# Splitting expert weights one expert ahead in a fused attention and mixture-of-experts block

## The reference

```python
xn = layernorm(x)                       # x: 4 x 256 tokens, 512 wide
# attention: 32 query heads, 8 key/value heads of 16
q, k, v = xn @ Wq, (xn @ Wkv) split in k and v, each shared by 4 heads
ctx = softmax(mask(q @ k.T) / 4) @ v
attn = ctx @ Wo + bo
# experts: 16 of inner width 256
scores = sigmoid(xn @ gate_w.T) + bias
cw = top-4 of scores, divided by their sum
z = silu(xn @ Wg[e].T) * (xn @ Wu[e].T) * cw[:, e]
out = sum over e of z @ Wd[e].T  +  shared expert
return x + attn + out
```

## Time and profile before

| | |
|---|---|
| median of 3 runs | 566.04 us (565.2 to 567.9) |
| the profiled execution | 569.64 us, span 567.9 us |
| mean granted clock of TensorE | 0.943 |
| busy TensorE, VectorE, ScalarE, GpSimd | 468.4, 365.0, 263.5, 268.3 us |

### The profile page before, as it was taken

The page is one execution under the profiler, slowest core; times in us unless marked ns, Lnnn a source line. Parts: engine busy times, 40 slices in busy tenths (PEclk is TensorE's granted clock), DMA queues, the critical chain, the costliest instruction groups (busy, mean ns, idle before and its releaser), DMA issues.

```text
span 567.9 us, 9993 instructions
## 1 busy us (share of the span) xinstructions
PE 468.4 (82%) x2968; PEld 344.9 (61%) x2968; DVE 365.0 (64%) x606; ACT 263.5 (46%) x386; POOL 268.3 (47%) x234
## 2 busy tenths in 40 slices
PE   0995789968989997789878878997978899889880
PEld 0964578846667775367656655765656557667650
DVE  7377874676567957375779871787775546766510
ACT  2531212216555655165668642655736335645610
POOL 2002593304764652267546863573757336364510
PEclk9997999987998998899999899998989999889976
DMA  7804963336666557465687883668655534334222
GB/s 285 329 28 111 226 231 100 107 118 214 158 130 152 113 104 212 142 157 96 141 236 190 277 162 60 154 139 205 175 104 107 95 56 83 68 54 81 38 38 37
DMA packets 32060, 78.23 MB, mean 138 GB/s; under 512 B 4288, under 2 KB 11200, under 8 KB 28800
## 3 DMA queue, kind: packets, MB, share of 16 engines
q0 software_dynamic: 11936, 27.53, 26.8%
q1 hardware_dynamic: 17808, 43.96, 23.5%
q10 hardware_dynamic: 2256, 6.03, 5.0%
HBM read 54.04 MB, written 23.33 MB: 136 GB/s over the span
## 4 chain that ended last, share of the span: by engine, by line
PE 45%; DVE 15%; issue 8%; DMA 8%; ACT 8%; ACTq 6%; POOL 5%; SPq 2%; DVEq 1%; POOLq 1%
PE psum L1093 24%; PE psum L1221 5%; DMA q_parts<-stage 3%; ACT wsplit L573 3%; DVE negm L906 3%; PE psum L1187 2%; PE psum L1203 2%; POOL xn L446 2%; PE psum L1058 2%; ACTq L266 2%; PE psum L1115 2%; PE psum L1042 2%; POOL out L457 1%; PE psum L1103 1%; ACTq L264 1%
## 5 line engine op out<-in xcount | busy, mean ns | idle before, releaser
L1093 PE MATMUL psum<-wsplit,xgT 128*128 (+1 forms) x660 | 175.0, 416 | 0.2
L1093 PEld LDWEIGHTS psum<-wsplit,xgT 128*128 128x128 f32 x660 | 125.8, 197 | 30.3 <-issue 2.7
L457 POOL DMA_INDIRECT out<-ysb,tab x48 | 88.6, 1845 | 105.1 <-ACT ysb L606 84.2
L1093 PE MATMUL psum<-wsplit,zT 128*128 (+1 forms) x336 | 95.3, 420 | 29.0 <-DVE zT L898 29.0
L1093 PEld LDWEIGHTS psum<-wsplit,zT 128*128 128x128 f32 x336 | 61.6, 193 | 48.9 <-issue 37.6
L948 DVE TENSOR_TENSOR xgT<-psum,xgT 128x512 fp32r<-128x512 f32 x47 | 32.3, 688 | 65.4 <-ACT xgT L569 65.3
L437 POOL DMA_INDIRECT xg<-xn_rows,tab x47 | 51.9, 1104 | 29.6 <-PE psum L1231 20.0
L648 ACT ACTIVATE xn<-psum 128x1536 f32<-128x1536 f32 x32 | 46.5, 1453 | 40.6 <-PE psum L1189 40.6
L975 DVE TENSOR_TENSOR plo<-xn,phi 128x1536 f16<-128x1536 f32 x32 | 63.5, 1984 | 1.0
L446 POOL TENSOR_SCALAR_AFFINE_SELECT xn<-xn 128x512 f32<-128x512 f32 x64 | 55.3, 1060 | 7.9 <-ACT xn L648 7.8
L462 POOL TENSOR_TENSOR wsplit<-wraw,wsplit (+1 forms) x16 | 39.1, 2446 | 41.1 <-ACT wsplit L573 41.1
(11 more groups left out here) (180 smaller groups left out, 655.9 us busy)
## 6 DMA issues: line engine op xcount, KB each, us to landing
wraw<-wexp SPq DMA_DIRECT2D x17, 1024.0 KB, 6.1
wraw<-wexp SPq DMA_DIRECT2D x17, 512.0 KB, 4.6
q_parts<-stage SPq DMA_DIRECT2D x16, 192.0 KB
q_pack<-q_parts ACTq DMA_DIRECT2D x6, 384.0 KB, 4.6
xn<-x SPq DMA_DIRECT2D x4, 512.0 KB, 5.2
xn_rows<-xn SPq DMA_DIRECT2D x8, 256.0 KB, 7.6
ctxs<-x SPq DMA_DIRECT2D x8, 256.0 KB, 3.2
out<-ysb SPq DMA_DIRECT2D x8, 256.0 KB, 3.2
```

Of the source, the lines that this page charges most:

```text
L457: nc.gpsimd.indirect_dma_start(out=out, out_offset=rows_of(s), in_=ysb[:, par, :], in_offset=None, compute_op=ALU.add).then_inc(y_out[par] ...
L1093: last = MM(dst, lhs(a, k), split_weights(place, w, c), start=m == 0, stop=m == len(products) - 1)
```

## The change

The gate/up weights of expert e + 1 are split in the first slot of expert e, not in the last slot before e + 1 begins; its down weights in the slot after that. On ScalarE the splits stand behind `y_evac`, on VectorE behind `low16`. The table now holds the number of the *next* expert at a slot that begins one, the place is worked out from that number, and each engine loads one register value a slot, after `tanh` or `gated`. On GpSimd, too, the register is loaded once. The transposed z goes to bank 3 (`ZB`), and the transposed maxima, after the first, to bank 4 (`NM`, the bank of `weighted`), so the wait for y moves from before `z_transpose` to before `down`, and three waits are added for the new sharing. Three small VectorE operations are added once, to make the table.

```diff
--- before.py
+++ after.py
@@ -250,6 +250,7 @@
 
 
         GU, XT, DN, PV = 5, 6, 7, 4
+        ZB, NM = 3, PV
         WO = (PV, 3)
         TRB = (0, 1, GU, XT)
 
@@ -462,13 +463,18 @@
                 nc.gpsimd.tensor_tensor(wsplit[:, place, 1, PARTS[1]], wraw[:, place, PARTS[1]],
                                         wsplit[:, place, 0, PARTS[1]].bitcast(F32), ALU.subtract).then_inc(w_low[1], 1)
 
-            def down_low_of(s):
-
-                number = pool.value_load(where[0:1, 2, s + 1:s + 2], min_val=0, max_val=NE)
-                with pool.If(number > 0):
-                    place = pool.value_load(where[0:1, 0, s + 1:s + 2], min_val=0, max_val=1)
-                    down_low(bass.ds(place, 1), number)
-                pool.end_ifs()
+            def first_of(s):
+
+                return pool.value_load(where[0:1, 2, s + 1:s + 2], min_val=0, max_val=NE)
+
+            def down_low_of(s, number):
+
+                if s == 1:
+                    down_low(1, 2)
+                elif s > 1:
+                    with pool.If(number > 0):
+                        down_low(bass.ds((number + 1) % 2, 1), number)
+                    pool.end_ifs()
 
             def add_attention(b):
                 pool.wait_ge(att_sb, QT * b + (QT + 1))
@@ -482,8 +488,10 @@
                     for j in BESIDE[g]:
                         if not (last and j + 3 >= SPS - 1):
                             gather(SPS * b + (j + 3), 1 - j % 2, SPS * b + (j + 2))
-                        if not (last and j == SPS - 1):
-                            down_low_of(SPS * b + j)
+                        s = SPS * b + j
+                        number = first_of(s - 1) if 1 < s < NSLOT else None
+                        if s < NSLOT:
+                            down_low_of(s, number)
                         add_rows(b, j)
                 add_attention(b)
 
@@ -559,7 +567,7 @@
                     act.wait_ge(z_done, n - 1)
                 S(th[:, par, :], bank(GU, FI), ACT.Tanh, scale=0.5).then_inc(th_done, 1)
 
-            def z_high(n, par, source=DN):
+            def z_high(n, par, source=ZB):
                 act.wait_ge(zt_ps, n + 1)
                 S(zT[:, par, 0, :, :], bank(source, FI).rearrange("p (k n) -> p k n", k=FK),
                   ACT.Copy).then_inc(zt_high, 1)
@@ -572,31 +580,30 @@
                 act.wait_ge(w_ready[part], number)
                 S(wsplit[:, place, 0, cols], wraw[:, place, cols], ACT.Copy).then_inc(w_high[part], 1)
 
-            def slot_parts(s, par, more):
-
-
-                if not more:
-                    z_high(s + (U1 - 1), par)
-                    return
-                number = act.value_load(where[0:1, 2, s + 2:s + 3], min_val=0, max_val=NE)
-                with act.If(number > 0):
-                    place = act.value_load(where[0:1, 0, s + 2:s + 3], min_val=0, max_val=1)
-                    x_high(s + 1, par)
-                    z_high(s + (U1 - 1), par)
-                    weights_high(bass.ds(place, 1), number, HALVES[0], 0)
-                    weights_high(bass.ds(place, 1), number, HALVES[1], 0)
-                with act.Else():
-                    x_high(s + 1, par)
-                    z_high(s + (U1 - 1), par)
-                act.end_ifs()
-
-            def down_high(s):
-
-                number = act.value_load(where[0:1, 2, s + 1:s + 2], min_val=0, max_val=NE)
-                with act.If(number > 0):
-                    place = act.value_load(where[0:1, 0, s + 1:s + 2], min_val=0, max_val=1)
-                    weights_high(bass.ds(place, 1), number, PARTS[1], 1)
-                act.end_ifs()
+            def first_of(s):
+
+                return act.value_load(where[0:1, 2, s + 1:s + 2], min_val=0, max_val=NE)
+
+            def gate_up_high(s, number):
+
+                if s == 0:
+                    weights_high(1, 2, HALVES[0], 0)
+                    weights_high(1, 2, HALVES[1], 0)
+                else:
+                    with act.If(number > 0):
+                        place = bass.ds((number + 1) % 2, 1)
+                        weights_high(place, number, HALVES[0], 0)
+                        weights_high(place, number, HALVES[1], 0)
+                    act.end_ifs()
+
+            def down_high(s, number):
+
+                if s == 1:
+                    weights_high(1, 2, PARTS[1], 1)
+                elif s > 1:
+                    with act.If(number > 0):
+                        weights_high(bass.ds((number + 1) % 2, 1), number, PARTS[1], 1)
+                    act.end_ifs()
 
             def y_evac(b, j):
 
@@ -621,7 +628,7 @@
             def minus_maxima(idx, half):
 
                 act.wait_ge(nmT_ps, idx + 1)
-                S(negmT[:, :], psum[0:MROWS * QT * H // 2, 3, 0:P], ACT.Copy).then_inc(nmT_sb, 1)
+                S(negmT[:, :], psum[0:MROWS * QT * H // 2, NM if idx else 3, 0:P], ACT.Copy).then_inc(nmT_sb, 1)
                 act.wait_ge(nmT_sb, idx + 1)
                 act.dma_start(q_pack[QROWS:QROWS + MROWS, H // 2 * half:H // 2 * (half + 1), :]
                               .rearrange("p h (q c) -> p (h q) c", q=QT),
@@ -658,27 +665,34 @@
                     act.wait_ge(ct_ps, QT * b + qt + 1)
                     S(ctxT[:, qt, :, :], bank(qt).rearrange("p (k n) -> p k n", k=KD), ACT.Copy).then_inc(ct_sb, 1)
 
-            def sequence(b, last):
+            def sequence(b, last, before):
                 for g in range(G):
                     numerators(b, g)
                     if g % 4 == 3 and not last:
                         pack_half(act, g // 4, b + 1)
                     for j in BESIDE[g]:
-                        s = SPS * b + j
-                        slot_parts(s, 1 - j % 2, not (last and j + 1 >= SPS - 1))
+                        s, par = SPS * b + j, j % 2
+                        if s + 1 < NSLOT:
+                            x_high(s + 1, 1 - par)
+                        z_high(s + (U1 - 1), 1 - par)
                         if j == BESIDE[g][-1] and (g == 3 or g == 7 and not last):
                             minus_maxima(2 * b + (g // 4 + 1), 1 - g // 4)
-                        if not (last and j == SPS - 1):
-                            tanh(s + U1, j % 2)
+                        if s < NSLOT:
+                            tanh(s + U1, par)
+                        number = first_of(s) if 0 < s < NSLOT else None
                         if j == BESIDE[g][0]:
                             high16(b, g)
-                        if not (last and j == SPS - 1):
-                            down_high(s)
                         y_evac(b, j)
+                        if s < NSLOT:
+                            gate_up_high(s, number)
+                            down_high(s, before)
+                        before = number
                 context_evac(b)
-
+                return before
+
+            before = None
             for b in range(B):
-                sequence(b, b == B - 1)
+                before = sequence(b, b == B - 1, before)
 
         @block.vector
         def _(dve):
@@ -857,7 +871,11 @@
                 own.did(V.tensor_scalar(where[:, 1, :], sexp_i[:, 0, :], 1.0, None, ALU.add))
                 own.did(V.memset(sexp_i[:, 1, 0:1], 0))
                 op(V.tensor_tensor(sexp_i[:, 1, 1:NCOL], sexp_i[:, 0, 1:NCOL], sexp_i[:, 0, 0:NCOL - 1], ALU.subtract))
-                V.tensor_tensor(where[:, 2, :], where[:, 1, :], sexp_i[:, 1, :], ALU.mult).then_inc(slots_known, 1)
+                own.did(V.tensor_scalar(sexp[:, 0, :], sexp[:, 1, :], float(NE - 1), None, ALU.is_lt))
+                own.wait()
+                op(V.scalar_tensor_tensor(out=sexp_i[:, 2, :], in0=sexp[:, 1, :], scalar=2.0, in1=sexp[:, 0, :],
+                                          op0=ALU.add, op1=ALU.mult))
+                V.tensor_tensor(where[:, 2, :], sexp_i[:, 2, :], sexp_i[:, 1, :], ALU.mult).then_inc(slots_known, 1)
 
 
             val = vg_sb[:, :, 0:G * HD].rearrange("p t (g d) -> p t g d", g=G)
@@ -893,7 +911,7 @@
                     dve.wait_ge(stored[n % 2], 16 * (n // 2))
                 V.tensor_tensor(ysb[:, n % 2, :], base[:, n % 2, :], bank(DN), ALU.add).then_inc(shared_done, 1)
 
-            def z_low(n, par, source=DN):
+            def z_low(n, par, source=ZB):
                 dve.wait_ge(zt_high, n + 1)
                 V.tensor_tensor(zT[:, par, 1, :, :], bank(source, FI).rearrange("p (k n) -> p k n", k=FK),
                                 zT[:, par, 0, :, :].bitcast(F32), ALU.subtract).then_inc(zt_sb, 1)
@@ -953,22 +971,20 @@
                 V.tensor_tensor(wsplit[:, place, 1, HALVES[half]], wraw[:, place, HALVES[half]],
                                 wsplit[:, place, 0, HALVES[half]].bitcast(F32), ALU.subtract).then_inc(w_low[0], 1)
 
-            def slot_parts(s, par, more):
-
-                if not more:
-                    z_low(s + (U1 - 1), par)
-                    return
```

(49 more changed lines are left out.)

## The result

The changed kernel takes 601.88 us (598.84 to 608.88, 4 runs) against 565.62 us of the kernel before (563.98 to 567.90): ratio 1.062 (1.055 to 1.069), slower by some 36 us. The ratios leave out executions that fell in a slower state of the chip, here the one of 608.88 us, so 1.062 is 600.65 against 565.62. The prediction was slower by 15.5 us, 567 to 592. The sign and the place were right, the size was not. The changed kernel was timed in the first group alone, and the others in later ones, so a difference between it and another kernel is known to 0.7 to 1 hundredth to either side.

The account below looks back on a forecast made before the run. TensorE, busy 82% of the span, was taken to set the pace. Terms 19.4 + 5.5 + 4.8 - 3.75 - 4.5 - 6.0 gave +15.5 us, from a median of 566.04 to 581.5 us, range 567 to 592.

Parts of the forecast that it names:

- The eight late splits: Before gate/up products after single-slot experts: the split comes last in the same slot and TensorE waits; +19.4 us.
- G+11.6: Slots with attention: earliest next gate/up start, 11.6 us after the slot's own: `low16` end 9.1, pair 2.36, semaphores about 0.15.
- Clock: TensorE's 1.2 GHz stretches behind gaps: five go or shrink (-7.0), five new before late gate/up products (+7.0); 0 taken.
- Port meetings: GpSimd's down low part beside VectorE's pair, slots 12, 19, 21, 22, 30: 2.4 us each, two of five taken, +4.8.
- VectorE's register load: Loads other than ScalarE's in packing slots: hidden under an executing instruction, worth nothing; without that cover at most 0.75 us a slot.
- the banks: z in its own bank: TensorE no longer waits for y before z's transposition; -4.5 us.
- `csum`, done a slot earlier: Before the transposition of the maxima: the new wait is for something already done a slot before; 0 us.
- ScalarE's load: Slots packing queries and keys: the load before `x_high` moves behind tanh; five slots at 0.75 us, -3.75 us.
- -6.0 us behind splits that left their slots: Where the split has left, `gated` and the transposed maxima's copy no longer stand behind it, so TensorE waits less; -6.0 us.
- likeliest case: Whole kernel: slower by 7 to 26 us, 573 to 592, with 581.5 as summed; chance 0.68.
- Rival D: Shared port decides: all five meetings cost 2.4 us (+7.2), two or three more low-clock stretches (+4); above 592, chance 0.07.

Follow-up runs that it names:

- scalar_early: The changed kernel with only ScalarE's splits moved back to their old place inside the slot, VectorE's left behind `low16`: 600.54 us, ratio 1.059.
- pair_before_maxima: The changed kernel with ScalarE's splits at the old place, VectorE's gate/up pair right behind `gated`, its register load before `gated`: 578.94 us, ratio 1.022.
- filled_waits: The changed kernel with 31 fp32 matmuls, results overwritten, in the seven places where TensorE waits for late gate/up low parts: 588.26 us, ratio 1.033.

## Why the prediction was partly right

**The eight late splits.** Right in mechanism and place: seven waits for the pair and one before the output projection. The waits were 31.4 us against a forecast of 20 to 25. scalar_early and pair_before_maxima show that VectorE's order is the cause, as the working of G+11.6 had it.

**Clock: the first step that failed, by its size.** The prediction said "I take **0**, bounds -7 and +7", since five dips would go and five come, at 1.4 us each. The half that goes was about right: besides slot 0's, which is slow in both kernels, five products of the kernel before took 3.44 to 4.59 us in place of 3.05, 5.8 us in all, and four of them are at full pace after; the fifth, slot 22's, now stands behind a late pair. The half that comes was priced at 7 us, by one product behind a gap of 2.89 us. Six products took 4.36 to 5.48 us, 12 us more in all, and filled_waits puts the new stretches at 16 us (11 to 22). So the term did not come to nothing but to some 6 us by the products alone, and 10 by filled_waits. The length of the wait does not give the price: 6.77 us was followed by 4.44, 4.02 by 5.48 and 3.28 by 3.06.

**Port meetings: the second, by their number.** They were taken as two of five, 4.8 us. Four of the five pairs paid: 4.49, 4.50, 4.50 and 4.53 us in slots 19, 21, 22 and 30, as the row of before with 3.84 for `low16` had said; in slot 12 the pair took 2.35 and GpSimd's split 3.02. With a shortened GpSimd the loss is 14 us smaller, which holds more than the port. The Trainium skill (SBUF — State Buffer, "SBUF: two separate sides") has the loser of the port fully blocked; the four pairs agree, at 2.1 us over 2.36 each.

**VectorE's register load: the third, an overlap that was not there.** It was costed at nothing under an executing instruction, and at most 0.75 us a slot "if that cover is gone"; that case was not put in the sum. The cover is missing behind `gated`: the load waits for its turn in the stream and the maxima behind it, 27 times and 8.5 us in all. It costs 1.1 hundredths, 6 us (1 to 12).

**The gains.** For the banks -4.5 us was forecast; alone they cost 0.4 hundredths, and with early splits nothing. The step "`csum`, done a slot earlier" did not hold as a wait that ends early: TensorE waits for `csum` in six places, though in the changed kernel this only takes the place of its waits for the split maxima there. For ScalarE's load -3.75 was forecast and none was found. Of the -6.0 us behind splits that left their slots little is seen: the waits for the DMA of the copied maxima fell from 2.8 us to nothing, but before `maxima_transpose` the sum stayed (7.1 and 7.5 us), and the waits before scores for the maxima grew from 5.7 to 7.4.

**The sum.** Forecast 15.5, measured 36, 20.5 more. It is these three steps that failed. The forecast had 7.0 for new dips of the clock, 4.8 for the port and 0 for the load, 11.8 in all; the three taken away together gave 31 us (29.5 by the medians as they stand), 19 more. That is nearly the whole miss. What is left is 4 us, and the forecast without these terms is 15.5 - 11.8 = 3.7. That this agrees is in part luck: at least 8.25 us of the gains in it (banks and ScalarE's load) were not found, so something else was forecast too dear by as much, and no run shows what. The likeliest case was right in sign, but its upper end of 592 had room for a clock of +7 or for five meetings, not for both and the load. Rival D had the port and the clock in it, at a chance of 0.07, with 4 us for the clock.

## What to carry to other kernels

Before moving work later in an engine's stream, ask whose wait it was filling: at the end of the slot, with their register loads, the splits cost 40 us more than in the place where VectorE waited for tanh. Look for the case in which "one ahead" is no step ahead at all; here half of the experts had one slot. And when the matmul engine gets new waits of several microseconds, price what follows them too, by a kernel that fills those waits with work whose result is not used: here it was some 16 of 36 us. Of the kernels tried, the splits one expert ahead at the old place inside the slot are the best, at 0.992 and 0.993 of the kernel before.

## What the runs showed of the hardware

A wait of 4.02 us before a product was followed by 5.48 us for twelve matmuls that take 3.06; with fp32 matmuls in the wait, and 0.58 us of idle time left, the same twelve took 3.06 us at a granted clock of 1.00. A kernel with 31 more matmuls was thus 2.7% faster (2.3% by the medians as they stand). Not each such wait had this price: behind the one of 3.28 us in slot 30 the twelve took 3.06. Two subtractions of VectorE with both inputs in SBUF took 4.49 to 4.53 us beside one of GpSimd, and 2.36 alone. And the load of a register in VectorE's stream left 0.21 us at the least and 0.86 at the most of idle time before the maxima, 27 times, where the instruction ahead of it was `gated`'s of 0.42 us; with the load before `gated` it left none.
